# Two attention phases of an encoder kernel get a new schedule: maxima in TensorE's row halves, small rows moved by DMA

## The reference

```python
q = (xq @ Wq).reshape(B, N, HEADS, D_HEAD)        # N = 512 queries
k = (xc @ Wk).reshape(B, S, HEADS, D_HEAD)        # S = 512 keys (self) or 1601 (cross)
v = (xc @ Wv).reshape(B, S, HEADS, D_HEAD)
scores = jnp.einsum('bnhd,bshd->bhns', q, k) * D_HEAD ** (-0.5)
attn = jax.nn.softmax(scores, axis=-1)
out = jnp.einsum('bhns,bshd->bnhd', attn, v).reshape(B, N, HEADS * D_HEAD)
return out @ Wo + bo
```

## Time and profile before

| What | Value |
|---|---|
| median of 3 runs | 3985.52 |
| the profiled execution's own time | 3982.79 |
| its span, first to last instruction | 3981.0 |
| PE busy | 3467.3 (87%) |
| DVE busy | 2430.2 (61%) |
| ACT busy | 2002.8 (50%) |
| POOL busy | 1124.5 (28%) |
| data moved by DMA | 590.63 MB, mean 148 GB/s |
| a0, first load issued to last store landed | 195.36 to 613.84 |
| a1, the same | 1019.33 to 2191.95 |

### The profile page before, as it was taken

One profiled execution on the slowest core, in us unless ns is written; L12 is line 12 of the kernel. 1 busy time (PEld: TensorE's weight loads), 2 busy tenths in 40 slices (PEclk: granted clock), 3 DMA queues, 4 the chain that ended last, 5 costly groups with the idle time before them and its releaser, 6 DMA issues. The chain is left out here.

```text
span 3981.0 us, 57943 instructions
## 1 busy us (share of the span) xinstructions
PE 3467.3 (87%) x17596; PEld 2014.2 (51%) x17596; DVE 2430.2 (61%) x4148; ACT 2002.8 (50%) x3541; POOL 1124.5 (28%) x539
## 2 busy tenths in 40 slices
PE   7899995999799999999999688588477599999776
PEld 5644444888455555555554466333356444444254
DVE  4368884343477777777776344386254399999333
ACT  4356662454255555555554233177244168888633
POOL 0056660000376666676666000012000000000000
PEclk9999997999799999999999898799799789999888
DMA  5787767999755555555551432244354522222121
GB/s 211 270 192 194 195 158 271 336 310 311 193 138 133 133 124 124 132 133 138 125 124 46 150 129 77 79 123 130 139 195 137 147 83 86 91 98 97 66 76 42
DMA packets 363424, 590.63 MB, mean 148 GB/s; under 512 B 43674, under 2 KB 196858, under 8 KB 362150
## 3 DMA queue, kind: packets, MB, share of 16 engines
q1 hardware_dynamic: 362312, 586.05, 50.8%
q10 hardware_dynamic: 958, 2.62, 0.3%
HBM read 345.71 MB, written 239.97 MB: 147 GB/s over the span
## 5 line engine op out<-in xcount | busy, mean ns | idle before, releaser
L1198 DVE TENSOR_REDUCE a_blk_max<-a_mx 128x1 f32<-128x402 f32 (+1 forms) x1280 | 734.2, 587 | 431.6 <-PE a_mx L1001 412.8
L1148 ACT ACTIVATE a_prob<-a_sc 128x512 f32<-128x512 f32 (+1 forms) x1088 | 640.1, 597 | 506.5 <-PE a_sc L1030 471.7
L1569 ACT ACTIVATE a_prob<-a_sc 128x512 f32<-128x512 f32 (+1 forms) x1088 | 585.6, 598 | 134.6 <-PE a_sc L1492 129.9
L977 POOL TENSOR_TENSOR a_prob_sum<-a_prob,a_prob_sum 128x1024 f32<-128x1024 f32 x256 | 617.3, 2412 | 63.6 <-ACT a_prob L1148 54.3
L1041 PE MATMUL a_pv<-a_prob,a_v 128*64 128x512 f32 (+1 forms) x2176 | 585.9, 617 | 0.0
L1596 DVE TENSOR_REDUCE a_blk_max<-a_mx 128x1 f32<-128x402 f32 x1024 | 512.3, 568 | 73.0 <-PE a_mx L1479 68.8
L1001 PE MATMUL a_mx<-a_k_stack,a_q_stack 128*128 128x402 f32 (+1 forms) x1280 | 485.0, 389 | 38.6 <-DMA a_q_stack<-q_hi_cross 23.4
L1029 PE MATMUL a_sc<-a_q_stack,a_k_stack 128*128 128x512 f32 (+1 forms) x1088 | 461.3, 424 | 2.1 <-ACT a_q_second L1131 2.1
L1030 PE MATMUL a_sc<-a_q_second,a_k_second 65*128 65x512 f32 (+1 forms) x1088 | 432.4, 397 | 0.0
L977 POOL TENSOR_TENSOR a_prob_sum<-a_prob 128x1024 f32<-128x1024 f32 x128 | 312.0, 2446 | 418.8 <-ACT a_prob L1148 418.8
L1001 PEld LDWEIGHTS a_mx<-a_k_stack,a_q_stack 128*128 128x128 f32 x1280 | 248.0, 194 | 292.2 <-DVE a_blk_max L1198 109.6
(11 more groups left out here) (248 smaller groups left out, 4895.9 us busy)
## 6 DMA issues: line engine op xcount, KB each, us to landing
a_v<-v_cross SPq DMA_DIRECT2D x48, 768.0 KB
a_k_stack<-k_hi_cross SPq DMA_DIRECT2D x32, 801.0 KB, 6.7
a_k_stack<-k_lo_cross SPq DMA_DIRECT2D x32, 801.0 KB, 9.8
a_k_second<-k_hi_cross SPq DMA_DIRECT2D x32, 801.0 KB
v_cross<-p_v_sb SPq DMA_DIRECT2D x48, 512.0 KB, 4.1
k_hi_cross<-p_split_hi SPq DMA_DIRECT2D x120, 200.0 KB, 3.2
k_lo_cross<-p_split_lo SPq DMA_DIRECT2D x120, 200.0 KB, 3.1
a_q_stack<-q_hi_self SPq DMA_DIRECT2D x64, 256.0 KB, 4.8
```

Of the source, the lines that this page charges most:

```text
L977: nc.gpsimd.tensor_tensor(prob_sum[:, h], prob_of(c, cp, h), other, ALU.add)\
L1148: nc.scalar.activation(prob_of(c, cp, h)[0:rows, k, :], sc[0:rows, (c * E + e) % SCB, :], ACT.Exp, scale=a.scale).then_inc(exp_done, 1)
L1198: nc.vector.reduce_max(blk_max[:, r, h, t, nb:nb + 1], mx[:, (c * NI + n) % MXB, 0:a.blk], AX.X)\
L1569: nc.scalar.activation(prob[0:keys, tau % RC, m, :], sc[0:keys, e % SCB, :], ACT.Exp, scale=a.scale).then_inc(exp_done, 1)
```

## The change

A new function `attend_wide` takes the place of `attend_phase` for a0 and a1. It is unrolled for all groups, and its clock is a window w: one pair of chunks for both heads. There are NCP windows a group, 2 in a0 and 7 in a1 (the last of the seven has one chunk).

- Maxima use q_hi k_hi alone: 64 rows a head, head 0 in the upper and head 1 in the lower row half, one matmul of each after the other. The k stack of head 1 is loaded with its halves swapped, which makes four k loads of 128 KB in place of two of 256 KB in a0.
- The maxima are laid out as columns, turned by DVE, stored to DRAM and loaded into one row of `q_second` by DMA. The row of ones becomes minus ones. The transposes on PE and the copies on ACT are gone.
- The sums of the exponentials come from 8 matmuls with the sums as weights and one column of ones moving. They go to an item bank, DVE takes reciprocals of 128x8, turns them, and DMA stores them and broadcasts them to 128 partitions (256 KB a group).
- PSUM has 4 item banks and 3 score banks in both phases, and no `aux`. The self attention has 5 slots for loads, the cross attention 3.

PE's order in a window, the order of SP's queue for a0, and the waits that they hold:

```diff
-        attend_phase(pr, "a0", SELF0)
+        attend_wide(pr, "a0", SELF0)
-        attend_phase(pr, "a1", CROSS0)
+        attend_wide(pr, "a1", CROSS0)
+    LEAD = 3
+    DEN_AT, DIVIDE_AT, HIGH_AT = NCP + 2, NCP + 5, NCP + 6
+    def pairs_by(w):
+        return min(NG * PAIRS, -(-PAIRS * (NCP + LEAD + w + 1) // NCP))
+            def store_maxima(n):
+                sp.wait_ge(turned, n + 1)
+                if n >= 2:
+                    sp.wait_ge(row_loaded[n % 2], 16 * (n // 2))
+                sp.dma_start(pr.maxima[n % 2].rearrange("c (b i) -> b c i", b=4), row_turned[:, n % 2, :])\
+                    .then_inc(max_stored[n % 2], 16)
+            def load_maxima(n):
+                sp.wait_ge(max_stored[n % 2], 16 * (n // 2 + 1))
+                sp.dma_start(words(q2[n % SLOTS][64:65]), pr.maxima[n % 2][0:8]...).then_inc(row_loaded[n % 2], 16)
+            def store_inverses(n):
+                sp.wait_ge(inv_turned, n + 1)
+                ...
+            def load_inverses(n):
+                sp.wait_ge(inv_stored[n % 2], 16 * (n // 2 + 1))
+                ...
+            for n in range(SLOTS - 1):
+                load_kq(n); load_second(n); load_v(n)
+                if n == 0:
+                    store_maxima(0); load_maxima(0)
+            for i in range(NG + 4):
+                if a.cross:
+                    at(load_kq, i + SLOTS - 1)
+                    at(load_second, i + SLOTS - 1)
+                    at(load_v, i + SLOTS - 1)
+                    at(store_inverses, i - 1)
+                    at(load_inverses, i - 1)
+                    at(store_maxima, i + 1)
+                    at(load_maxima, i + 1)
+                    at(store, i - 1)
+                else:
+                    at(store_maxima, i + 1)
+                    at(load_maxima, i + 1)
+                    at(load_kq, i + SLOTS - 1)
+                    at(load_second, i + SLOTS - 1)
+                    at(load_v, i + SLOTS - 1)
+                    at(store_inverses, i - 2)
+                    at(load_inverses, i - 2)
+                    at(store, i - 4)
+            def maxima(p0, p1):
+                for p in range(p0, p1):
+                    ...
+                    for h in range(2):
+                        n = 2 * place(p) + h
+                        if n >= MXB:
+                            pe.wait_ge(item_read, n - MXB + 1)
+                        rows, at = slice(64 * h, 64 * h + 64), a.block_at[nb]
+                        nc.tensor.matmul(mx[:, n % MXB, 0:a.blk], qst[i % SLOTS][rows, h, t * P:(t + 1) * P],
+                                         kst[i % SLOTS][rows, h, at:at + a.blk], start=True, stop=True)\
+                            .then_inc(item_done, 1)
+            def denominators(i):
+                n = 2 * den_place(i)
+                pe.wait_ge(merged, 2 * (i + 1))
+                pe.wait_ge(item_read, n - MXB + 1)
+                for h in range(2):
+                    for t in range(4):
+                        c = 4 * h + t
+                        last = nc.tensor.matmul(mx[:, n % MXB, c:c + 1], chunk_sum[:, h, t * P:(t + 1) * P],
+                                                pr.ones[:, 0:1], start=True, stop=True)
+                last.then_inc(den_done, 1)
+            maxima(0, pairs_by(-1))
+            for w in range(T):
+                for ch in a.pair(w % NCP):
+                    for h in range(2):
+                        scores(w, ch % 2, h)
+                sums_at(w)
+                maxima(pairs_by(w - 1), pairs_by(w))
+                if w:
+                    values(w - 1)
```

More of the change, by code:

```diff
@@ L107, in __init__ @@
             self.o[a.name] = [dram(f"o_{p}_{a.name}", [a.NG, P, NQ], F32) for p in ("hi", "lo")]
-        self.maxima = [dram(f"maxima{n}", [P, 32], F32) for n in range(2)]
-        self.inverse = [dram(f"inverse{n}", [4, NQ], F32) for n in range(2)]
+        self.maxima = [dram(f"maxima{n}", [32, P], F32) for n in range(2)]
+        self.inverse = [dram(f"inverse{n}", [32, P], F32) for n in range(2)]
         self.vec = self.sbuf("vectors", [P, NVEC], F32)
@@ L1379, in store_maxima @@
                     sp.wait_ge(row_loaded[n % 2], 16 * (n // 2))
-                sp.dma_start(pr.maxima[n % 2], row_turned[:, n % 2, :]).then_inc(max_stored[n % 2], 16)
+                sp.dma_start(pr.maxima[n % 2].rearrange("c (b i) -> b c i", b=4), row_turned[:, n % 2, :])\
+                    .then_inc(max_stored[n % 2], 16)
             def load_maxima(n):
                 sp.wait_ge(max_stored[n % 2], 16 * (n // 2 + 1))
-                dst = qst[n % SLOTS][63:P:64].rearrange("p j (t b i) -> p (j t) b i", t=4, b=4)
-                src = pr.maxima[n % 2].rearrange("(b x c) i -> x c b i", x=4, c=8)
-                sp.dma_start(words(dst), src[0:2]).then_inc(row_loaded[n % 2], 16)
+                sp.dma_start(words(qst[n % SLOTS][63:P:64]),
+                             pr.maxima[n % 2][0:16].rearrange("(r j t) i -> r j (t i)", r=2, j=2))\
+                    .then_inc(row_loaded[n % 2], 16)
             def load_sums(n):
@@ L1397, in store_inverses @@
                     sp.wait_ge(inv_loaded[(n - 2) % OS], 16 * ((n - 2) // OS + 1))
-                sp.dma_start(pr.inverse[n % 2].rearrange("h (x i) -> (h x) i", x=32), den[:, n % OS, :])\
+                sp.dma_start(pr.inverse[n % 2][0:16].rearrange("c (y i) -> (c y) i", i=16), den[:, n % OS, :])\
                     .then_inc(inv_stored, 16)
@@ L1404, in load_inverses @@
                     sp.wait_ge(divided, n - OS + 1)
-                sp.dma_start(inv[:, n % OS, :], pr.inverse[n % 2].rearrange("(h u) n -> h u n", u=1)
-                             .to_broadcast([4, 32, NQ])).then_inc(inv_loaded[n % OS], 16)
+                rows = pr.inverse[n % 2][0:16].rearrange("(h u c) i -> h u (c i)", h=4, u=1)
+                sp.dma_start(inv[:, n % OS, :], rows.to_broadcast([4, 32, NQ])).then_inc(inv_loaded[n % OS], 16)
             def store(n):
```

720 lines of the change are left out of this document (285 added, 435 removed).

## The result

The changed kernel takes 4396.5 us (median of 4, 4373.0 to 4421.5) against 3983.8 of the kernel before on the same chip: 1.103 times as long, 95% interval 1.1006 to 1.1058. The direction was right and the size was not: +115 us was predicted in a0 and -3 in a1, and they were +261 and +175, which is 436 of the 439 us between the two spans. The other phases together account for the remaining 3.

A forecast was written before the change was run, and what follows sets the result against it. SP's DMA queue was to bound a0 at 16.0 us a group and PE a1 at 34.6. From 3982.8 us, +115 in a0 and -3 in a1 gave 4095, range 3990 to 4150 at 0.79.

The forecast's parts named there:

- PE's sum: PE's work per group: 34.6 us in a1 with waits, against 35.26 before; 11.5 us in a0, against 12.18.
- third pair's wait: In a1, PE waits for DVE to read the burst's earlier maxima: 1.15 us each, 2.3 us a group.
- the 0.8 us for DVE's last sums: In a1, PE reaches the denominators at 6.3 us but DVE's additions last until 7.0: 0.8 us a group.
- The starts: Time before the first score: 31 us in a0 against 12.5 before; 50 us in a1 against 30.5.
- SP's round in a0: SP's single DMA queue, with small stores landing behind earlier transfers, repeats every 16.0 us a group, against PE's 11.5.
- 256 KB of inverses stand ahead too, 0.7 us at 384 GB/s: In a0, the broadcast inverses' share of the 5.2 us from loading inverses to the maxima's landing.
- the bound of 17.2 us: Upper bound on SP's a0 round, using the 4.5 us landing from the earlier trace.
- The range: Whole kernel: 4040 to 4145 us for the forecast at 0.62; 3990 to 4150 at 0.79 with rivals included.
- a1's clock: PE in a1 was priced at full clock, with no term for a lower one.
- rival 3: In a0, idling PE may restart at lower clock and DVE pass delay on: 2 us more a group, 4155 or more; chance 0.10.
- Rival 2: In a0, small stores don't wait for loads; SP's round is 11.5 us at most, kernel 3978 us; chance 0.15.
- The sign given for it: Rival 2 decides wherever a small store lands under about 5 us behind 1.84 MB of loads.

The follow-up runs named there:

- row denominators: Changed kernel with denominators by two matmuls as rows, reciprocals on DVE and no inverses by DMA, denominators placed behind the window's maxima: 4138.3 us.
- later multiplication: Changed kernel with DVE's multiplication by the inverses two windows later in a1, and a0's small DMAs on ACT's queue: 4248.2 us.
- one sum of eight: Changed kernel with one denominator matmul in place of eight in a1; in a0 split broadcast and both small stores ahead of both small loads: 4197.7 us.
- second queue: Changed kernel with a0's small DMAs on ACT's queue, split broadcast, and in a1 spread pairs and multiplication two windows later: 4083.5 us.

## Why the prediction was wrong in size

- *PE's sum* held, in part by luck: a group of a1 is some 34.5 us at full clock (34.6), a0's stream 11.3 (11.5). The third pair's wait was sized well: a window with it lasts 6.00 us (1606.00 to 1612.00), one without 4.61, so 1.39 for the predicted 1.15 and the pair's own 0.2. But a full window takes 4.61 for the predicted 4.35, some 1.6 us a group. Against that the denominators take 1.87 with their border (1636.56 to 1638.43) for 2.5 with theirs and a wait, and the 0.8 us for DVE's last sums hardly occurred (4 times in all of a1). Two small slips of arithmetic change nothing: a1's terms add up to -2, not -3, and three groups at 11.5 behind 480 end at 514.5, not 516.
- *The starts* held: a0's first score comes after 32.6 us (228.94 less 196.30; predicted 31), a1's after 51.1 (1336.43 less 1285.36; predicted 50).
- *SP's round in a0.* The mechanism was right: two small stores a round, each landing when the queue before it has drained. The step that failed is "256 KB of inverses stand ahead too, 0.7 us at 384 GB/s". I priced the broadcast by the bytes and the rate of the earlier trace rows, as if it used sixteen engines. It ran at the share of two and added 4.8 us a round. The split broadcast shows it by itself: 21.0 to 16.2 us, 134 us over the phase, which is nearly all of the 146 us by which a0 was missed. The rate of a DMA was taken from one with another access pattern; the bound of 17.2 us came from the same rows and could not contain it.
- *The range* left this out as well. A bound from above for a form of DMA that the trace before doesn't show should have come from the slowest form in it, not from the nearest in bytes.
- *a1's clock* is the larger failure, a term put at nothing. The 34.6 us a group have PE at clock 1.00 since the earlier trace rows has 1.00 in mid-phase, and rival 3 brings a lower clock up for a0 alone. The runs showed 0.87, which cost 39.7 less 34.5, 5.2 us a group: by estimate 150 to 165 of the 178 us by which a1 was missed. The rest wasn't taken apart.
- *What lowers it in a1* is shown as to places: behind the third pair's wait in a group's first window, and behind the sixteen short matmuls. Undoing the row halves, spreading the pairs, or moving the third pairs by one window each empty the first place, or all but empty it, and bring the clock from 0.87 to 0.96 or 0.97; row denominators (with the order that came with them) empty the second and bring it to 0.91; both together give 1.00. The later multiplication alone doesn't move it, and one sum of eight traded the second place for waits for ACT. Why the same wait of 0.48 us lowers the clock in the first window and not in others isn't shown; nor is what the two places have in common.
- *Rival 2* (small stores that don't wait) is refuted by the rounds, 21.0 and 16.2 us where it had 11.5 at most, and by the second queue's gain of 55 us. The sign given for it was a poor one: the store of the inverses did land 4.85 us after its issue (516.61 to 521.46), "under about 5 us", but it is issued 5.8 us after the first load, so that this is the predicted 10.2.
- *Rival 3* was right in kind: a0's clock is 0.70 over the phase. It stood at 0.10 beside the forecast, though it is no alternative to it but an addition, and it didn't reach a1, where the clock cost most.

## To carry to other kernels

Price every new DMA by how many DMA engines its access pattern reaches before its bytes, and every small DMA by what stands ahead of it in its queue; a queue of its own costs another engine a few issues a group and takes the wait away. Where PE bounds at full clock, put the clock into the sum: multiply each group's time by its clock to see whether an edit changed the work or the clock, look up what PE did right before each fall, and distrust a saving on PE that comes with new waits or with short matmuls. A test that takes one suspect away must be checked for new waits before it clears it. And before an operation of DVE is moved to fill a gap, look at what POOL is doing there.

## What the runs showed of the hardware

- A DMA whose pattern is 2 x 64 partitions ran at a DMA share of 0.12 to 0.13 and 33 to 44 GB/s; as two DMAs of 64 partitions each the round was 4.8 us shorter. The Trainium skill (DMA: Bandwidth & Descriptors, Why a DMA increments its semaphore by 16) states it: the number of engines is the largest up to 16 that divides the slowest dimension on both sides. The trace agrees (2 of 16 is 0.125), and applied beforehand the rule would have given the missing term.
- DVE's multiplication of two operands in SBUF lasted 0.68 us alone, 0.97 on average in a1 before, 2.86 and 4.84 us beside POOL's sums, and the last two ended 0.55 us behind an instruction of POOL (472.88 to 473.43 and 1628.55 to 1629.10). The Trainium skill (SBUF — State Buffer, SBUF: two separate sides) describes an exclusive lock on a shared port pair for a DVE instruction with two SBUF inputs and a GpSimd instruction that reads SBUF; the ends right behind POOL's agree with it.
- The granted clock fell to 0.50 (1.2 GHz) in stretches where PE was recorded as busy 100% of the time, behind sixteen matmuls of one column, and in others behind waits of 0.5 to 1.3 us. A busy share of PE near 1 doesn't show that the clock holds.
